# Zero fill in parts, weights in pairs, fetches that add on landing: one change to a routed MLP beside window attention

## What is computed

```python
xn = _layernorm(x, axis=-1)
# attention: qkv = tok @ qkv_w; two halves of 8 channels, windows of 8 tokens, 3-tap conv on v
att = concat([x1, x2]) @ proj_w + proj_b
tok = tok + layernorm(att) * ln_w + ln_b          # then transposed back
# experts: sigmoid gate, 2 of 4 groups, 6 of 16 experts, weights normalised times 2.5
for e in range(E):
    out = out + comb[:, e:e+1] * ((silu(hs @ gate_proj[e].T) * (hs @ up_proj[e].T)) @ down_proj[e].T)
shared = (silu(xn @ sg.T) * (xn @ su.T)) @ sd.T
return x + attention(xn) + out + shared
```

## Time and profile before

| | us |
|---|---|
| median of 3 runs | 500.22 (497.48 to 501.37) |
| the profiled execution | 500.93 |
| its span, first to last instruction | 499.1 |
| mean granted clock of TensorE | 0.913 |

### The profile page before, as it was taken

The page is one execution under the profiler, slowest core; times in us unless marked ns, Lnnn a source line. Parts: engine busy times, 40 slices in busy tenths (PEclk is TensorE's granted clock), DMA queues, the critical chain, the costliest instruction groups (busy, mean ns, idle before and its releaser), DMA issues.

```text
span 499.1 us, 7322 instructions
## 1 busy us (share of the span) xinstructions
PE 415.1 (83%) x1981; PEld 318.4 (64%) x1981; DVE 361.3 (72%) x585; ACT 224.7 (45%) x609; POOL 237.3 (48%) x223
## 2 busy tenths in 40 slices
PE   5599987998377999989899999999999999998000
PEld 5597976777255777767667777767766677676000
DVE  2537693277469999999899998999943255589831
ACT  3445323224325444554466665664456544644000
POOL 2611212475767777777200000006377777575772
PEclk9596988899779999999899999999999999999555
DMA  7999999324245666655333323336467996563633
GB/s 193 338 350 351 362 414 367 109 91 167 90 156 168 207 201 213 195 185 168 100 99 97 110 87 106 103 98 172 142 180 204 248 237 177 161 185 115 193 109 87
DMA packets 65733, 91.55 MB, mean 183 GB/s; under 512 B 8224, under 2 KB 57120, under 8 KB 65440
## 3 DMA queue, kind: packets, MB, share of 16 engines
q1 hardware_dynamic: 53920, 63.02, 40.8%
q0 software_dynamic: 9216, 25.96, 17.1%
q10 hardware_dynamic: 2560, 2.10, 1.6%
HBM read 43.48 MB, written 47.57 MB: 182 GB/s over the span
## 4 chain that ended last, share of the span: by engine, by line
PE 48%; DVE 18%; DMA 13%; issue 7%; POOL 6%; ACT 4%; SPq 2%; DVEq 1%; POOLq 0%
PE gate L897 17%; PE ps_y L920 15%; DMA xs_dram<-xrow,slot_i 11%; PE up L887 3%; POOL xs_dram L536 3%; PE ps_y L913 3%; DVE prod L996 3%; DVE qkv L996 3%; PE misc L947 2%; PE gate L833 2%; DVE inter_s L1407 1%; DVE yacc L1489 1%; DVE sc L996 1%; SPq L381 1%; PE up L833 1%
## 5 line engine op out<-in xcount | busy, mean ns | idle before, releaser
L897 PE MATMUL gate<-wrec,xgT 128*128 x444 | 152.4, 466 | 0.9 <-issue 0.6
L536 POOL DMA_INDIRECT xs_dram<-xrow,slot_i x96 | 112.3, 1169 | 60.4 <-DMA xs_dram<-xrow,slot_i 31.0
L920 PE MATMUL ps_y<-wrec,interT 88*128 x444 | 119.2, 391 | 9.0 <-ACT interT L667 4.5
L555 POOL DMA_INDIRECT gat<-y_dram,slot_i x57 | 64.4, 1129 | 130.1 <-DMA y_dram<-y_s 98.5
L920 PEld LDWEIGHTS ps_y<-wrec,interT 88*128 88x128 f32 x444 | 81.1, 190 | 50.9 <-issue 31.1
L897 PEld LDWEIGHTS gate<-wrec,xgT 128*128 128x128 f32 x444 | 76.7, 193 | 26.2 <-issue 2.9
L1407 DVE SCALAR_TENSOR_TENSOR inter_s<-gate,xg,gate_s 128x176 f32<-128x176 f32 x111 | 43.7, 394 | 41.1 <-ACT gate_s L660 35.4
L680 ACT ACTIVATE y_s<-ps_y 128x256 f32<-128x256 f32 x107 | 41.1, 384 | 69.2 <-PE ps_y L920 67.7
L660 ACT ACTIVATE gate_s<-gate 128x176 f32<-128x176 f32 x111 | 35.2, 318 | 62.4 <-PE gate L897 61.8
L887 PE MATMUL up<-ident,xg 128*128 128x128 f32 x222 | 43.5, 277 | 11.9 <-DMA xg<-xs_dram 11.9
L887 PEld LDWEIGHTS up<-ident,xg 128*128 128x128 f32 x222 | 31.6, 143 | 24.1 <-DMA xg<-xs_dram 12.6
(11 more groups left out here) (198 smaller groups left out, 626.7 us busy)
## 6 DMA issues: line engine op xcount, KB each, us to landing
xs_dram<-zrow SPq DMA_DIRECT2D x1, 15096.0 KB, 50.9
xg<-xs_dram SPq DMA_DIRECT2D x111, 136.0 KB, 2.4
y_dram<-y_s SPq DMA_DIRECT2D x111, 128.0 KB, 1.7
wrec<-wexp SPq DMA_DIRECT2D x14, 608.0 KB, 14.4
xn_dram<-xrow SPq DMA_DIRECT2D x8, 256.0 KB, 10.1
qkv<-xn_dram SPq DMA_DIRECT2D x8, 256.0 KB, 4.9
xs_dram<-xrow,slot_i POOLq DMA_INDIRECT x96, 2.9
wrec<-wexp SPq DMA_DIRECT2D x1, 1216.0 KB, 5.8
```

Of the source, the lines that this page charges most:

```text
L536: nc.gpsimd.indirect_dma_start(xs_dram, bass.IndirectOffsetOnAxis(slot_i[:, o:o + 1], 0), xw[:, c, :], None).then_inc(sent[n % LANES], 16)
L555: nc.gpsimd.indirect_dma_start(places[place_of(n)][:, there:there + H], None, y_dram[0:DONE[max(d for d in DONE if d <= first)] * P, :], b ...
L897: last = nc.tensor.matmul(guA[t % 2][:, 0:2 * I], xgT[:, t % 2, k * P:(k + 1) * P], wrec[:, bass.ds(record + k * 2 * I, 2 * I)], start=(k ...
L920: last = nc.tensor.matmul(ps_y[:, t % 2 * 2 * H:t % 2 * 2 * H + H], interT[:, t % 2, k * P:(k + 1) * P], wrec[0:HALF, bass.ds(record + KT ...
```

## The change

- **Zeros in parts.** SP fills tiles 0 to 68 of `xs_dram` with one DMA and a small DRAM table `z_dram` of three tiles with another. Tiles 69 to 86 are filled by 6 copies of `z_dram` (3 tiles, 408 KB each) behind units 8 to 10, tiles 87 to 110 by 8 such copies in SP's turns 4 to 11 of the tile loop. Scatters wait for the part that they write: the first 54 for the first, the next 18 for the 6 copies, the rest for the last 8.
- **Weights in pairs.** The 14 loads no longer stand behind the fill at once: two follow each `m_ok` of units 2 to 8.
- **Normalised rows.** The 8 stores to `xn_dram` go from ahead of the tiles to SP's turns 19 to 26.
- **Jobs.** PE does all qkv jobs before it waits for tile 0 (before, the last one stood behind `columns(0)`).
- **Attention's end.** Transposes of the last quarter, the reading back of rows, projections and `normalise` each come one or two tiles earlier (85, 85, 89, 98).
- **Fetches.** For columns 0 to 11 the 72 fetches are DMAs that add to `yacc` on landing, 54 for columns 0 to 8 with 5 in flight, then 18 for columns 9 to 11 with 3. They have no place and no sum on DVE. The 24 of columns 12 to 15 stay plain, each with a place of its own; 6 of their 18 sums stand at tiles 105 to 107, the others behind the tiles.

```diff
-XN_AT = 87
-PROJECTIONS_AT = {91 + j: (j,) for j in range(8)}
-NORM_AT = 100
-GROUPS = ((0, 3), (3, 6), (6, 9), (9, 12), (12, 14), (14, 15), (15, 16))
-    ADD_AT.setdefault((77 if _n < 9 else 78) + 14 * _n // 9, []).append(_n)
+XN_AT = 85
+XN_OUT_AT = 19
+ZEROS_AT = 4
+ZT = 3
+PROJECTIONS_AT = {89 + j: (j,) for j in range(8)}
+NORM_AT = 98
+SUMMED = ((0, 9), (9, 12))
+PLAIN = ((12, 14), (14, 15), (15, 16))
+FLIGHT_BACK = (5, 3)
+ADD_AT = {105 + n // 2: (n, n + 1) for n in range(0, TOP, 2)}
...
-            for e in range(TAIL):
-                sp.dma_start(wrec[:, e * REC:(e + 1) * REC], wexp[:, e * REC:(e + 1) * REC]).then_inc(w_in, 16)
-            sp.wait_ge(xn_ok, C)
-            for run, b, r in lane_runs():
-                sp.dma_start(by_lane(xn_dram, b, r), xw[run, :, 0:H]).then_inc(xn_out, 16)
+            zero_tiles(sp, 0, DONE[0], first_zeros)
+            sp.dma_start(z_dram.rearrange("(t p) w -> p t w", p=P), zrow[:, :].unsqueeze(1).to_broadcast([P, ZT, XW])
+                         ).then_inc(spare_zeros, 16)
+            for u in range(2, 2 + TAIL // 2):
+                sp.wait_ge(m_ok, u + 1)
+                for e in (2 * u - 4, 2 * u - 3):
+                    sp.dma_start(wrec[:, e * REC:(e + 1) * REC], wexp[:, e * REC:(e + 1) * REC]).then_inc(w_in, 16)
+            sp.wait_ge(spare_zeros, 16)
+            for n, t in enumerate(range(DONE[0], DONE[MARKS[1]], ZT)):
+                sp.wait_ge(m_ok, 2 + TAIL // 2 + n // 2)
+                copy_zeros(sp, t, more_zeros)
...
+                if t - ZEROS_AT in range(0, (NT - DONE[MARKS[1]]) // ZT):
+                    copy_zeros(sp, DONE[MARKS[1]] + (t - ZEROS_AT) * ZT, last_zeros)
+                if t - XN_OUT_AT in range(2 * 4):
+                    run, b, r = lane_runs()[t - XN_OUT_AT]
+                    sp.dma_start(by_lane(xn_dram, b, r), xw[run, :, 0:H]).then_inc(xn_out, 16)
...
-            pool.wait_ge(fill_out, 16)
+            pool.wait_ge(first_zeros, 16)
...
+            for (first, last), back in zip(SUMMED, FLIGHT_BACK):
+                stored(first)
+                order = [(c, k) for k in range(TOP) for c in range(first, last)]
+                for n, (c, k) in enumerate(order):
+                    if n >= back:
+                        before, choice = order[n - back]
+                        pool.wait_ge(summed[before], 16 * (choice + 1))
+                    rows, offsets = rows_of(c, k)
+                    nc.gpsimd.indirect_dma_start(yacc[:, c * H:(c + 1) * H], None, rows, offsets, compute_op=ALU.add
+                                                 ).then_inc(summed[c], 16)
+            pool.wait_ge(att_ok, 2 * B)
             for n, (first, last, k) in enumerate(FETCHES):
...
                 qkv_job(n)
-                if n == QKV_JOBS - 2:
-                    columns(0)
+            columns(0)
             columns(1)
...
                     settle()
-                    dve.wait_ge(added, sums.value())
+                    for c in range(TILES * b, min(TILES * b + TILES, PLAIN[0][0])):
+                        dve.wait_ge(summed[c], 16 * TOP)
+                    if sums.value():
+                        dve.wait_ge(added, sums.value())
```

More of the change, by code:

```diff
@@ L102 @@
 TRANSPOSES_AT = {50: (0,), 51: (1,), 52: (2,), 53: (3,), 54: (4,), 55: (5,), 56: (6,), 57: (7,),
-                 86: (8, 9), 87: (10, 11), 88: (12, 13), 89: (14, 15)}
-XN_AT = 87
-PROJECTIONS_AT = {91 + j: (j,) for j in range(8)}
-NORM_AT = 100
-GROUPS = ((0, 3), (3, 6), (6, 9), (9, 12), (12, 14), (14, 15), (15, 16))
[L111 to L115, removed]
-    ADD_AT.setdefault((77 if _n < 9 else 78) + 14 * _n // 9, []).append(_n)
[L119 to L133, removed]
+                 85: (8, 9), 86: (10, 11), 87: (12, 13), 88: (14, 15)}
+XN_AT = 85
[7 more added lines that the diff above has]
+FLIGHT_BACK = (5, 3)
+FETCHES = tuple((first, last, k) for first, last in PLAIN for k in range(TOP))
+ADD_AT = {105 + n // 2: (n, n + 1) for n in range(0, TOP, 2)}
 def quota_until(t):
@@ L291, in build @@
         put = [sem(f"put{i}") for i in range(YRING)]
-        got = [sem(f"got{i}") for i in range(PLACES)]
+        summed = [sem(f"summed{c}") for c in range(PLAIN[0][0])]
+        got = [sem(f"got{i}") for i in range(len(FETCHES))]
         added = sem("added")
@@ L343, in by_lane @@
             return table[ROWS * b:ROWS * (b + 1), :].rearrange("(c r) w -> r c w", c=C)[r]
[L346 removed]
+        places = [gat[:, i * 2 * H:(i + 1) * 2 * H] for i in range(4)] + [sc[:, 0:2 * H], prod[:, 0, H:3 * H]]
+        places += [gat[:, 8 * H:9 * H], sc[:, 2 * H:3 * H], prod[:, 0, 3 * H:4 * H]] + [prod[:, 1, n * H:n * H + H] for n in range(1, 4)]
+        places += [gat[:, i * H:(i + 1) * H] for i in range(TOP)]
         def bank(n):
@@ L387, in store_out @@
             engine.wait_ge(norm_ok, (c1 - 1) // TILES + 1)
-            engine.wait_ge(added, TOP * sum(first < c1 for first, _ in GROUPS))
+            if c1 > PLAIN[0][0]:
+                engine.wait_ge(added, TOP * sum(first < c1 for first, _ in PLAIN))
             for run, b_of, r in lane_runs():
@@ L1483, in add_results @@
                 acc = yacc[:, first * H:last * H]
-                dve.wait_ge(got[place_of(n)], 16 * fetched(n))
+                dve.wait_ge(got[n], 16 * (last - first))
                 if sums.value():
@@ L1488, in add_results @@
                     dve.wait_ge(norm_ok, parts.value())
-                nc.vector.tensor_tensor(acc, acc, places[place_of(n)][:, 0:(last - first) * H], ALU.add).then_inc(added, 1)
+                nc.vector.tensor_tensor(acc, acc, places[n], ALU.add).then_inc(added, 1)
                 sums.add()
@@ L1543, in _ @@
             assert next(heads, None) is None
-            for i, _ in enumerate(late):
-                if i % 2:
-                    add_results(sums.value())
+            for _ in late:
+                pass
             for n in range(sums.value(), len(FETCHES)):
```

46 lines of the change are left out of this document (30 added, 16 removed).

## The result

The changed kernel takes 546.74 us (median of 4 runs, 543.81 to 548.79) against 499.41 of the kernel before beside it: a ratio of 1.094, 95% interval 1.087 to 1.101. It is 47 us slower where 18 less were predicted. The profiled execution took 543.81 us, its span is 542.1.

A forecast was written before the change was run, and what follows sets the result against it. DVE was taken to bound the attention, PE 393 to 430 us, POOL and DVE the return. Front -0.3, attention -0.5, new wait +2.2 and tail -19.2 took the span from 499.1 to 481.3; time 482.4 us, range 475 to 499.

The forecast's parts named there:

- the price of the adding fetch: POOL's return: each of the 72 adding fetches takes 1.33 us, as scatters and plain fetches do while DVE is busy.
- The bounds, 1.25 and 2.84: Limits for one adding fetch on POOL: 1.25 us as a plain fetch in quiet, 2.84 as scatters under load.
- adding fetches are slow: Rival at the 72 DMAs ahead of fetch 84: at 1.58 us each nothing gained, at 1.8 end at 515; chance 0.23.
- the term for late scatters in the tile loop: Attention stage: scatters start 3 us later against the tiles but mostly catch up; 1.0 us lost (0 to 6).
- the price of a busy microsecond: Front, scatters 1 to 30: 0.8 us lost per microsecond of burst, 3.0 for the last weights; scatter 30 at 137.3.
- bursts harmless: Rival at the front: bursts do not hurt scatters, scatter 30 at 123 to 126, end 9 lower at 473; chance 0.12.
- tile 0: Front: with jobs first, tile 0's product follows scatter 30 by 4.7 + 3.8 us, at 145.8, a gain of 0.3.
- the attention stage: Tile loop's last tiles: three DVE sums leave where DVE sets the pace; 1.5 us gained, between 0 and 2.8.
- the tail: From the last product to the end: 23.6 us instead of 42.8, so 19.2 less.

The follow-up runs named there:

- forms: The changed kernel with fetches of choices 2 to 5 bringing 64 of 128 rows, those of choices 4 and 5 not adding; 513.19 us in a single execution.
- plain_fetches: The changed kernel with the 72 fetches overwriting `yacc` instead of adding to it; 502.33 us, ratio to before 1.010.

## Why the prediction was wrong

**The step that failed is the price of the adding fetch.** "I take 1.33 as for scatters and fetches while DVE is busy, since the rows and their number are the same": a plain fetch there took 1.316 (1.27 without the wait for stores), an adding one 1.97. The bounds, 1.25 and 2.84, held it. The step from the price to the end was right. By the text the end is 29 us behind the landing of fetch 84; it landed at 508.31 + 2.80 = 511.11, and the end by that is 540.1, measured 542.1. Put together: fetch 84 went 58.8 us later than forecast (508.31 for 449.5), of these 11.5 by the late first fetch (350.92 for 339.4), 72 x (1.974 - 1.33) = 46.4 by the price, 0.9 by the eleven behind. The rival "adding fetches are slow" names place, price and the point from which it decides, 1.58, and its line "at 1.8 it ends at 515" goes on to 1.97. It was given 0.23. What spoke against it, that issue time goes by the number of rows, came from two kinds of DMA neither of which adds; for the third kind no row spoke at all, and a choice near the lower bound of 1.25 to 2.84 was not one that the rows made.

**The second failure is the term for late scatters in the tile loop**: 1.0 us taken (0 to 6), 9.7 measured. The argument was that scatters take 1.33 where their brake allows one in 1.55, so they catch up. That held for landings of 2.9 us. They were 4.0, and scatters 30 to 96 took 113.4 us instead of 104.0. SP's timeline at tile 15 shows the wait, and what was queued behind it:

```profile
175.93 0.47 SPq L375 DMA_DIRECT2D xs_dram<-z_dram  x1
182.59 0.32 SPq L448 DMA_DIRECT2D xg<-xs_dram  x1
182.97 0.42 SPq L453 DMA_DIRECT2D y_dram<-y_s  x1
183.43 0.47 SPq L375 DMA_DIRECT2D xs_dram<-z_dram  x1
```

The load of tile 15 (`xg` in SP's turn 11, behind 54 scatters) goes 6.2 us behind the copy ahead of it; a store and the last zero copy wait behind it. At tile 39 the same happens with scatter 96: issued at 251.57, landed 2.64 later, the tile loaded at 256.44, PE's transposes at 256.49. Together the prediction had the place right ("tile 15 needs 54 scatters and tile 39 all 96") and the size wrong. That part alone would have moved the forecast to 491.

Landings are not the whole of the 9.4 us. By POOL's timeline its idle time ahead of scatters 31 to 96 grew from 26.6 to 32.7 us, and its issues of scatters 30 to 95 from 77.2 to 80.6. The idle time goes with the front: 32.1 to 35.8 us in the six executions that have the whole of it on the ordinary chips with two in flight, 24.9 to 26.9 in three with that of before. The issues do not: 71.8 to 82.2 us, whatever the front. In forms they take 72.2, 8.4 less than in the changed kernel, and that is most of the 10 us by which scatter 96 goes earlier there. The long ones stand beside DVE's attention, in step with its products of tiles (two engines' timelines of the changed kernel):

```profile
241.13 2.27 POOL L557 DMA_INDIRECT xs_dram<-xrow,slot_i  x1 [0.31 <-issue]
243.71 2.27 POOL L557 DMA_INDIRECT xs_dram<-xrow,slot_i  x1 [0.30 <-issue]
```

```profile
242.49 0.39 DVE L1444 SCALAR_TENSOR_TENSOR inter_s<-gate,xg,gate_s 128x176 f32<-128x176 f32 x1
245.07 0.39 DVE L1444 SCALAR_TENSOR_TENSOR inter_s<-gate,xg,gate_s 128x176 f32<-128x176 f32 x1
```

Six scatters in a row go 2.58 us apart, as the products do, and five so in the kernel before (227.62 to 237.93); the 1.33 that the prediction read from 15 scatters is of a stretch without them.

**Right: scatter 30, by the price of a busy microsecond.** Forecast 137.3, measured 138.17; the other five executions with this front and two in flight have 137.16 to 141.04, so that it came within a microsecond is luck in part. The chain of waits shows the landings:

```profile
79.51 6.28 DMA xs_dram<-xrow,slot_i
...
102.97 7.68 DMA xs_dram<-xrow,slot_i
...
138.17 2.42 DMA xs_dram<-xrow,slot_i
```

Those beside pairs and copies took up to 7.68 us, the last 2.42. In the window from 97 to 107, which lies in the pairs, the DMA engines are busy 0.93 and move 316 GB/s. The rival "bursts harmless" (123 to 126) fell: the landings have a median of 4.8 us from 74 to 126, of 2.5 from 126 to 150. The Trainium skill (DMA: Bandwidth & Descriptors, Queues, rings and completion order) has each DMA engine take turns between its rows packet by packet, by which the prediction estimated that a small scatter loses about its own length to a burst, 0.34 us. The trace disagrees with that estimate, with 2.3 us more in the median; what makes a landing longer is not shown. The DMA issues of the page after (KB, us to landing):

```profile
xs_dram<-zrow SPq DMA_DIRECT2D x1, 9384.0 KB, 33.9
wrec<-wexp SPq DMA_DIRECT2D x14, 608.0 KB, 5.1
xs_dram<-z_dram SPq DMA_DIRECT2D x14, 408.0 KB, 5.9
...
xs_dram<-xrow,slot_i POOLq DMA_INDIRECT x96, 3.9
```

**Half right: tile 0.** 145.8 forecast, 148.07 measured. Jobs first took DVE's work out of the way as said, and left PE without work: it idled 14.46 us, and the window from 137 to 147 has a granted clock of 0.50, that is 1.2 GHz. Four products took 2.71 us where the earlier trace rows has 2.21, and two tiles' transposes came ahead of them in one row, 1.26. With scatter 30's 0.9 this makes 2.0 of the 2.3.

**Right: the attention stage and the tail.** Tiles 77 to 105 gained 1.1 (1.5 forecast). The tail from the last product lasts 24.4 (23.6 forecast; 42.8 before). It is true that the last fetch is now only 15.7 us behind the last product (33.3 before): it is so because the product now waits for the fetches. A tail measured from the last product says nothing of the whole when that product stands behind the same queue.

**Still open.** Whether the landings in the tile loop need all parts together to reach 4 us is not shown, nor why the issues beside DVE are long in one execution and short in another. Nor is it shown whether 128-row adding fetches of fewer columns, only as many as POOL can issue before tile 105, would pay: between fetch 1 and the product of tile 105 there is room for (454.63 - 350.92) / 1.97 = 52 of them and no other. That was not tried.

## What to carry to other kernels

An operation that takes work off one engine costs on the engine that issues it, and a kind that the trace doesn't hold has no price near its neighbours: take the break-even price first (here 1.58 against 1.33) and let the forecast's chance hang on it. Before a sum is moved into the DMA, look at what holds its queue up; here the waits for places went when the sums stood at the tiles where their data had landed. What a large DMA does to small ones beside it is best judged by the landing times of the small ones in its stretch, stretch by stretch. And executions of one kernel differ: with the same front scatter 96 went at anything from 241.57 to 256.43, so a part that moves it by a few microseconds wants more than one trace, and all parts on one chip.

## What the runs showed of the hardware

- A DMA with an index list that adds on landing takes POOL 1.54 us to issue in quiet, one that doesn't 0.95; with 64 rows 1.41 and 0.90. Its landing took 4.5 us in the median, the plain one's 3.3.
- An adding DMA of 128 rows has 144 packets in the queue of POOL's DMAs, a plain one of the same bytes 48 (16128 and 9216 in all, the changed kernel and plain_fetches).
- Beside DVE's attention eight of the first nine adding ones took 2.26 to 2.35 us, 2.58 apart, and one beside `normalise` 2.89. In plain_fetches, beside the same operations of DVE, the plain ones took at most 1.14. But the slowdown does not belong to the form that adds: plain scatters took 2.27 us at the same pace, six in the changed kernel and five in the kernel before. That DVE's load is its cause was not tested.
- Small scatters of 139 KB landed in 2.4 us in quiet and in up to 8.7 beside weights in pairs and zero copies.
- On another chip the same kernel before took 534 us instead of 497, with weight loads of PE idle for 67 and 71 us, no releaser shown, in the two kernels profiled there; in the kernel before as profiled first it was 31.
